# Self-attention with plain values and an output projection over all tokens, and the first cross attention's transposes of P by quarters

## The reference, cut to what matters

```
# layer 0, 16 heads of width 8, keys and values from a context of 77 rows
scores = einsum(Q, K) / 8**0.5, causal;  sim = softmax(scores);  att = einsum(sim, V)
x = LN(att + q);  x = x + gelu(x @ W1.T + b1) @ W2.T + b2

# layer 3, 16 heads of width 64
xn = rms_norm(x, attn_norm_w)
q, k, v = split(xn @ to_qkv_w);  q, k = rope(q), rope(k)
kf = [memory keys (16 equal ones), 16 persistent keys, k];  vf likewise
mask: a token sees memory and persistent keys, and the tokens before it in its own segment of 64
o = softmax(q kf^T / 8) vf
x = x + concat_heads(o) @ to_out_w          # 1024 x 128
```

## Time and profile before

| | us |
|---|---|
| median of 3 runs | 2436.97 (2435.53 to 2437.94) |
| the profiled execution | 2442.62 |
| its span in the profile | 2440.8 |

### The profile page before, as it was taken

One profiled execution on the slowest core, in us unless ns is written; L12 is line 12 of the kernel. 1 busy time (PEld: TensorE's weight loads), 2 busy tenths in 40 slices (PEclk: granted clock), 3 DMA queues, 4 the chain that ended last, 5 costly groups with the idle time before them and its releaser, 6 DMA issues.

```text
span 2440.8 us, 83677 instructions
## 1 busy us (share of the span) xinstructions
PE 2287.5 (94%) x27182; PEld 1807.3 (74%) x27182; DVE 1872.0 (77%) x4067; ACT 1474.2 (60%) x3344; POOL 1562.2 (64%) x2374
## 2 busy tenths in 40 slices
PE   7999999988888888999999979999999999999899
PEld 5777778976666666777778967777777777777688
DVE  5888882149999996777775678888888888888566
ACT  5777775548888886888885524444444444444443
POOL 2666663119999995666667766666666666666433
PEclk9999999979999998999999989999999999999999
DMA  4111112235555552222222223333333333333221
GB/s 128 43 43 43 43 45 63 71 90 167 168 167 168 167 157 47 52 50 52 52 50 58 69 72 93 94 96 97 95 94 95 94 94 94 94 94 93 61 62 54
DMA packets 443188, 211.72 MB, mean 87 GB/s; under 512 B 206672, under 2 KB 434000, under 8 KB 442960
## 3 DMA queue, kind: packets, MB, share of 16 engines
q1 hardware_dynamic: 443088, 210.43, 31.9%
HBM read 113.28 MB, written 29.88 MB: 59 GB/s over the span
## 4 chain that ended last, share of the span: by engine, by line
PE 70%; POOL 12%; issue 8%; ACT 4%; DVE 2%; SPq 1%; DMA 1%; POOLq 0%; DVEq 0%; ACTq 0%
PE bank L685 10%; PE bank L1458 9%; PE bank L1418 9%; PE bank L1149 6%; PE bank L702 5%; PE bank L1486 5%; PE bank L659 4%; PE bank L1163 4%; POOL sb_region L1008 4%; ACT sb_pT L771 3%; PE bank L1468 3%; PE bank L1444 3%; POOL sb_rstd L1025 2%; PE bank L1494 2%; POOL sb_z L1029 2%
## 5 line engine op out<-in xcount | busy, mean ns | idle before, releaser
L685 PE MATMUL bank<-sb_ident,sb_region 128*77 128x128 f32 x3072 | 413.0, 278 | 54.0 <-ACT sb_pT L771 50.7
L771 ACT ACTIVATE sb_pT<-bank 77x1024 f32<-77x1024 f32 x384 | 391.8, 1020 | 83.3 <-PE bank L685 82.5
L685 PEld LDWEIGHTS bank<-sb_ident,sb_region 128*77 128x77 f32 x3072 | 349.8, 151 | 107.7 <-issue 104.0
L1548 ACT ACTIVATE sb_l<-sb_l 128x640 f32<-128x640 f32 x128 | 94.5, 738 | 386.6 <-DVE sb_l L1596 386.6
L862 DVE TENSOR_REDUCE sb_max<-bank 128x8 f32<-128x616 f32 x256 | 203.4, 795 | 143.3 <-PE bank L667 74.5
L766 ACT ACTIVATE sb_region<-sb_region 128x616 f32<-128x616 f32 x384 | 276.6, 721 | 22.3 <-POOL sb_region L1008 20.7
L1675 POOL TENSOR_TENSOR sb_pn<-sb_l,sb_r_all 128x512 f32<-128x512 f32 x128 | 134.8, 1053 | 233.0 <-DVE sb_r_all L1606 222.0
L1418 PE MATMUL bank<-sb_region,sb_wqkv 128*128 128x128 f32 x2048 | 253.5, 277 | 6.2 <-DVE sb_region L1584 5.5
L1418 PEld LDWEIGHTS bank<-sb_region,sb_wqkv 128*128 128x128 f32 x2048 | 241.8, 194 | 8.8 <-DVE sb_region L1584 6.1
L1458 PE MATMUL bank<-sb_wvo,sb_region 128*64 128x512 f32 x1024 | 247.9, 605 | 0.0
L867 DVE TENSOR_TENSOR sb_region<-bank,sb_max 128x616 f32<-128x616 f32 x256 | 204.8, 800 | 11.7
(11 more groups left out here) (181 smaller groups left out, 5434.6 us busy)
## 6 DMA issues: line engine op xcount, KB each, us to landing
sb_region<-in_side SPq DMA_DIRECT2D x64, 616.0 KB, 3.8
sb_pT<-sb_region SPq DMA_DIRECT2D x512, 64.0 KB, 2.0
sb_kF<-sb_region SPq DMA_DIRECT2D x512, 64.0 KB, 2.1
scratch_after_A<-sb_y SPq DMA_DIRECT2D x256, 64.0 KB, 1.7
sb_fx<-scratch_after_A SPq DMA_DIRECT2D x96, 128.0 KB, 2.1
sb_mask<-in_mask SPq DMA_DIRECT2D x64, 154.0 KB, 2.3
sb_x<-scratch_after_F SPq DMA_DIRECT2D x128, 64.0 KB, 1.9
sb_ctx<-in_ctxT SPq DMA_DIRECT2D x192, 38.5 KB, 1.8
```

Of the source, the lines that this page charges most:

```text
L685: mm = nc.tensor.transpose(two[0:C, h * T:(h + 1) * T], p_s[b.par][:, head * C:(head + 1) * C], ident[:])
L771: nc.scalar.activation(pT_s[k][:], two[0:C, :], ACT.Copy).then_inc(pT_kept.sem(b), 1)
```

## The change

**A3.** The values are no longer folded with the output weights. `values` is now v = xn Wv for one segment g of all 16 heads: two matmuls of 512 columns in a half instead of four. `attend_local` multiplies v with transposed P for every head and segment apart: 16 matmuls of 64 rows, 64 weight columns and 64 moving columns, into banks 0 and 1, and gives O^T. ACT copies it (`keep_outputs`), and `project_local` multiplies it with `wout3`, in four matmuls over all 128 tokens that accumulate in `out3_bank`. The heads of the two row groups of an odd c land in the other half of the partitions, and so `wout3_turned`, loaded once, holds those rows turned. The output of a half is now taken one half later (the project of (b-1, h) stands in the step of (b, h)). The rope's banks are 3 and 6 instead of 0 and 1. The triangle mask is added by two matmuls over all 128 rows of output instead of four. The norm's weight is applied when xT is copied; SP loads `vom` and the residual for b instead of b+1 and stores y of b-2 instead of b-1.

**The memory stage** loses the eight transposes of Wv, both `fold_values`, and DVE's copies of them. **A0**: each half of P is transposed and copied by quarters of four heads, each quarter in a bank of its own with semaphores `quarter_made` and `quarter_kept`. A1 and A2 keep the halves.

```
@@ events
-        pT_made = event("pT_made", CROSS, parts=2)
-        pT_kept = event("pT_kept", CROSS, parts=2)
+        pT_made = event("pT_made", CROSS[1:], parts=2)
+        pT_kept = event("pT_kept", CROSS[1:], parts=2)
+        quarter_made = event("quarter_made", ["A0"], parts=4)
+        quarter_kept = event("quarter_kept", ["A0"], parts=4)
@@ A0, PE
+            def transpose_quarters(b, k):
+                pe.wait_ge(exp_made.sem(b), exp_made.count(ph, b, k))
+                for q in range(2):
+                    old, old_k = (b, 0) if k == 1 else (b + -1, 1)
+                    if old.exists:
+                        pe.wait_ge(quarter_kept.sem(old), quarter_kept.count(ph, old, 2 * old_k + q))
+                    for h in range(QH):
+                        head = (2 * k + q) * QH + h
+                        mm = nc.tensor.transpose(bank[4 + q][0:C, h * T:(h + 1) * T], p_s[b.par][:, head * C:(head + 1) * C], ident[:])
+                    mm.then_inc(quarter_made.sem(b), 1)
@@ A0, ACT
+            def keep_quarters(b, k):
+                wait_earlier(act, att_made, ph, b, 1, k)
+                for q in range(2):
+                    act.wait_ge(quarter_made.sem(b), quarter_made.count(ph, b, 2 * k + q))
+                    nc.scalar.activation(pT_s[k][:, q * QH * T:(q + 1) * QH * T], bank[4 + q][0:C, :], ACT.Copy).then_inc(quarter_kept.sem(b), 1)
@@ A3, banks
-        rope_bank = bank[0:2]
+        rope_bank = (bank[3], bank[6])
-        vo_banks = (bank[6], bank[3])
+        oT3_banks, v3_bank = bank[0:2], bank[1]
@@ A3, SP
-                if has(1):
-                    load_vom(b + 1)
-                    load_residual(b + 1)
-                if has(-1):
-                    sp.wait_ge(out3_taken.sem(b + -1), out3_taken.count(ph3, b + -1, 1))
+                if has(0):
+                    load_vom(b)
+                    load_residual(b)
+                if has(-2):
+                    sp.wait_ge(out3_taken.sem(b + -2), out3_taken.count(ph3, b + -2, 1))
@@ A3, PE
+            def values(b, g, first):
+                done, done_h = (b + -2, 1) if g == 0 else (b + -1, 0)
+                if done.exists:
+                    pe.wait_ge(oT3_kept.sem(done), oT3_kept.count(ph3, done, done_h))
...
                 for r in range(2):
-                    mm = nc.tensor.matmul(vo_banks[g][r * SEG:(r + 1) * SEG, :], xnT_s[b.lap][:, g * SEG:(g + 1) * SEG],
-                                          wvo[:, (2 * h + r) * HC * D:(2 * h + r + 1) * HC * D], start=True, stop=True)
+                    mm = nc.tensor.matmul(v3_bank[r * SEG:(r + 1) * SEG, :], xnT_s[b.lap][:, g * SEG:(g + 1) * SEG], wv3[:, r], start=True, stop=True)
+            def outputs_ready(b, h, held):
+                for v, g in held:
+                    pe.wait_ge(v3_kept.sem(v), v3_kept.count(ph3, v, g))
+            def attend_local(b, h):
+                for c in range(HC):
+                    for r in range(2):
+                        rows = slice(r * KH, (r + 1) * KH)
+                        side = (r + c) % 2
+                        for g in range(T // SEG):
+                            tok, col, out = c * T + g * SEG, (g * (H // 2) + h * HC + c) * KH, (c // 2 * 2 + g) * SEG
+                            mm = nc.tensor.matmul(oT3_banks[c % 2][side * KH:(side + 1) * KH, out:out + SEG], v3_s[b.par][rows, col:col + KH],
+                                                  pT_s3[h][rows, tok:tok + SEG], start=True, stop=True)
+                mm.then_inc(oT3_made.sem(b), 1)
+            def project_local(b, h, leaving):
...
+                if leaving:
+                    late, late_h = (b, 1) if h == 0 else (b + 1, 0)
+                    pe.wait_ge(pp3_kept.sem(late), pp3_kept.count(ph3, late, late_h))
...
                 for c in range(HC):
+                    weights = wout3[:, h * HC + c, :] if c % 2 == 0 else wout3_turned[:, (h * HC + c) // 2, :]
+                    tok = (c % 2 * (HC // 2) + c // 2) * T
+                    nc.tensor.matmul(out3_bank[:, 0:D], oT3_s[h][:, tok:tok + T], weights, start=(c == 0), stop=False, skip_group_check=True)
@@ A3, ACT
             def step(b, has):
                 for h in range(2):
+                    if has(-1):
+                        keep_outputs(b + -1, h)
                     if has(0):
                         exps(b, h)
                     if has(-1) if h == 0 else has(0):
                         keep_p(*half_before(b, h))
-                    if has(0):
-                        keep_values(b, h, 0)
-                        keep_values(b, h, 1)
+                    if has(0) if h == 0 else has(1):
+                        keep_values(b + h, 1 - h)
@@ memory stage, PE
-            for c in range(H // 2):
-                col = 2 * HD3 + c * 128
-                mm = nc.tensor.transpose(bank[4 + c // 4][:, (c % 4) * 128:(c % 4 + 1) * 128], wqkv[:, col:col + 128], ident[:])
-            pe.wait_ge(wvT_kept, 2)
-            fold_values(0)
-            pe.wait_ge(wvo_kept, 1)
-            fold_values(1)
```

More of the change, by code:

```diff
@@ L1413, in project @@
                 for eo in range(2):
+                    if b.first and what == "q" and eo == 1:
+                        last = Batch(GROUPS // 2 - 1, 1)
+                        pe.wait_ge(ft_made.sem(last), ft_made.count("F2", last))
                     if old.exists:
@@ L1511, in step @@
                         project(b + 2, "qk"[h])
-                    if has(0):
-                        values(b, h, 0)
-                        values(b, h, 1)
-                    if leaving:
-                        attend_local(old, old_h)
+                    if has(0) if h == 0 else has(1):
+                        values(b + h, 1 - h, not has(-1))
+                    if has(-1):
+                        project_local(b + -1, h, leaving)
                     following = (b, 1) if h == 0 else (b + 1, 0)
@@ L1633, in step @@
                 for h in range(2):
-                    if has(-1):
-                        take_out(b + -1, h)
+                    if has(-2) if h == 0 else has(-1):
+                        take_out(*((b + -2, 1) if h == 0 else (b + -1, 0)))
                     if h == 0 and has(3):
@@ L1730, in build_layers @@
         rest = [(dst[:], src) for dst, src in consts]
+        by_row = a[p + "to_out_w"].rearrange("(c odd r v) d -> odd r v c d", odd=2, r=2, v=KH)
+        for r in range(2):
+            rest.append((wout3_turned[r * KH:(r + 1) * KH, :, :], by_row[1, 1 - r]))
         for r in range(2):
```

140 lines of the change are left out of this document (68 added, 72 removed).

## The result

The changed kernel takes 2527.99 us (median of 3 runs, 2523.56 to 2532.52) against 2436.97 us (2435.53 to 2437.94): ratio 1.0364, 95% interval 1.0344 to 1.0384. It is 91 us slower where 32 us faster was forecast, and outside of the range. Its profiled execution has a span of 2526.2 us.

The account below looks back on a forecast made before the run. TensorE's own work was taken to bound A3, with SP next, and waits and a POOL chain A0. A3 -16.5, A0 -12.5, memory stage -5, A1 and A2 +2 sum to -32 us: median 2405, range 2388 to 2428.

Parts of the forecast that it names:

- The failed step: A3: TensorE's own work sets the time, so each microsecond taken from it counts 64 times until something else is late.
- Rival (1): A3: a run of four on one tile in attend_local holds the queue, 1.48 us, 2501 in all; chance 8%.
- Rival (3): A3 gains next to nothing, as v3_kept or the late rope puts back 0.15 us per half; 2422; chance 17%.
- A3's own gain: Self-attention: 13.03 us per batch, 0.30 less, for 62 batches, -18.5, plus 2 at the end: -16.5 us.
- The deeper pipeline's tail: End of A3: the last half's copy (0.60) and projection (0.94) stand bare with their latencies: +2 us.
- The wait on pp3_kept stays covered by 0.3: A3, per half: values end at 4.97 us, the transposed persistent part is kept at 4.67, so no wait.
- The rope and v3_kept: A3: the rope's 0.46 us delay fits DVE's 0.54 idle; project_local's 0.94 covers the 0.92 v3_kept wait, almost bare.
- A0: First cross attention: quarters remove the transposes' wait; the scores-to-scores chain over POOL sets 5.38 us, 0.2 less per batch: -12.5 us.
- The memory stage: Both folds go: -3.3 us for the first, -1.5 for the second, together -5, bounds -8 and -2.
- A1 and A2: Second and third cross attention: same work, two more register instructions per batch on ACT in each: +2 us, bounds 0 and +6.
- SP's 12.98: A3: SP issues 20 DMAs per batch in 12.98 us and can't go much lower, the next limit after TensorE.
- Same-bank pairs: A3, attend_local: row tiles writing one PSUM bank take turns, 0.95 us, 2433 in all; a rival at 6%.

Follow-up runs that it names:

- slot 0: Changed kernel with only TensorE's code moved, the self-attention loop's head at the first of a block's 256 instruction places: 2425.06 us, ratio 0.9937 to the kernel before.
- the run without waits: Changed kernel at slot 0, ScalarE's copies of the transposed probabilities put ahead of the exponentials: 2420.30 us, ratio 0.9912 to the kernel before.
- the run with the hint: Changed kernel, loop not placed, with a hint at the body's head announcing its closing branch to the instruction fetch: 2422.84 us, ratio 0.9916 to the kernel before.
- the last version: Changed kernel with branch hint, probability copies ahead of exponentials, and the self-attention mask again in four pieces of 64 partitions: 2417.19 us, ratio 0.9911 to the kernel before.
- slots 0 and 88: Changed kernel with only the loop's head placed, at instruction 0 or 88 of a block: 2425.06 and 2424.34 us, ratios 0.9937 and 0.9934 to the kernel before.
- slot 104: Changed kernel with only the loop's head placed, at instruction 104 of a block: 2468.71 us, ratio 1.0075 to the kernel before.
- the lengthened old one: Kernel before plus 14 superfluous matmuls per self-attention half: 2489.55 us (1.0191) with the loop's head at slot 0, 2584.02 us (1.0573) at slot 239.

## Why the prediction was wrong

**The failed step** is in the part on A3, and it is one that is not there. It says "each microsecond taken from it counts 64 times, until something else is late", and lists as what could be late SP, ScalarE's copies and the ropes. The instructions themselves are not in the list. The change's count of records was worked out for their duration (32 for attend_local, 8 for the projection, half of the values) and never added up as code. The sum was at hand: 170 records per batch before are 170 products and as many weight loads, and 36 more of each come to 72 x 4 = 288 instructions per pass, on top of 1,427 (the trace has 269 more, since other instructions fell away). What the profile before would have shown is its queue list: 57 code packets in all, none in A3's passes, so the loop was being replayed from what the engine holds. How much it holds no row before shows. The Trainium skill does, in Runtime: NRT & Kernel Launch, section Instruction fetch mechanics: 128 KiB for TensorE, 2,048 instructions, refilled in blocks of 16 KiB, and a taken branch to a block outside of a window of two stops the engine until that block is fetched. The runs agree with the capacity and the block: 7 blocks are held, 8 are at the edge. They disagree with the window of two blocks: at slot 0 a body of 7 blocks is replayed for 12 passes without a packet. By the capacity the changed loop with its 1,696 instructions would have looked safe; that it isn't hangs on where its head stands.

What the runs showed in the place of that step: the loop's code is fetched anew in every pass, at 8.6 us per pass, and the same operations at slot 0 take 2425.06 us where they took 2527.99, 103 us less. That is still outside of the range: 17 us under the kernel before and not 32, for the sizes told of next.

**Rival (1)**, slower by a run of four in attend_local (2501), had the sign and not the mechanism: attend_local takes 0.69 us. **Rival (3)**, A3 gains next to nothing (2422), has about the time of the runs without fetches, by chance: neither v3_kept nor the ropes took the gain.

**A3's own gain**, apart from the fetches, was forecast as -16.5 and is about zero. Three sizes were off. (a) Per half, values and attention together were to go from 2.74 to 2.57; the sections of the run without waits are 0.687 for attend_local (0.70 forecast), 1.009 for half of the values (0.89), 0.995 for the projection (0.94): 2.69. The values' four records cost 0.25 each and not 0.22, and the first two of the projection 0.33 and not 0.22. Both stand at a change of tile shape, for which I had 0.04 in all, and only for another place; no run changes the shape alone, so that this is the cause is a reading. (b) The new mask, two pieces for four, was put at nothing: 0.215 + 0.611 for mask and scores against 0.133 + 0.664, 0.03 more per half. Against this the persistent part (L1493 and L1494 before) fell from 0.97 to 0.81 us per batch, which the sum didn't have. In all TensorE's own work fell from 13.31 to 13.12 us per batch where 12.99 was forecast. So a pass is 52.5 to 52.7 instead of 4 x 13.03 = 52.1, and 12 passes gain 5.6 us. (c) The deeper pipeline's tail was to cost 2 and costs 4 to 5. TensorE's waits in it in the run with the hint (2194 to 2307), in total, times, longest:

```profile
PE bank L1541 <- ACT sb_ppT L1603: 3.3, 2, 2.2
PE bank L1541 <- ACT sb_ppT L1605: 3.2, 3, 1.2
PE bank L1508 <- issue: 1.7, 1, 1.7
```

The copies of the persistent part stop TensorE for 6.5 us against 4.9 before, and the stop for code is the 1.7. At slot 0 the copies are 6.0, and two more stops (3.3 in all) stand in front of L1546, where the code waits for SP's gathers. In the last version the end of A3 takes 7.8 us more than before, 3.5 of them in one wait for gathered keys.

**The covers.** "The wait on pp3_kept stays covered by 0.3" was wrong: in the run at slot 0 the copy lands 0.05 before the projection starts, and TensorE waits for it in both halves, 0.05 us per batch in all. The rope and v3_kept did hold, with no wait of TensorE on either.

**A0** was right in mechanism and nearly in size: -12.5 forecast, -13.9 measured alone, by the closed chain over POOL. In the traces a pass of four batches went from 22.06 to 21.22 us, 0.21 less per batch, for 0.2; the levels are both 0.1 under those of the prediction, since the trace has somewhat fewer records than the program. **The memory stage**: -5 forecast, -5.9 measured (-5.3 from its first matmul to A1's first). **A1 and A2**: +2 forecast, +1.5 measured. **SP's 12.98** was right as a floor, though in the loop only the last run reaches it.

**Same-bank pairs.** The rule that was weighed against L667 does not hold for this pattern: attend_local writes one bank from two row groups, and takes 0.69 us and not the 0.95 of turns.

## What to carry to other kernels

Count the instructions of a loop's body on each engine, weight loads included, before and after a change that trades a few long operations for many short ones, and look at the instruction queue's row: a loop that is replayed without a packet has a property that can be lost. If TensorE has idle time marked "issue" once per pass, directly behind the loop's branch, and the queue that brings the code has packets in every pass, it is the code and not the data. "Issue" alone is not the mark: the stops at L1546 had it and were waits for gathered keys. The place of the loop's head took the stops away here without touching an operation, and so did a hint for its branch. Short matmuls of another tile shape seem to have a price at each change of shape (here about 0.1 us), which can eat what fewer columns bring.

## What the runs showed of the hardware that was not expected

- TensorE replayed a body of 1,696 instructions from what it holds when this lay in 7 blocks of 256 (slots 0 and 88), fetched all of it in 5 of 12 passes when it reached 8 slots into an eighth (slot 104), and in every pass where it reached 147 slots into it (the head at slot 243 by the distance of the two stops). One block too many costs all blocks.
- The cost was 8.6 us per pass of 52.7 in the changed kernel and 8.2 in the lengthened old one: in the pass shown two stops of 3.4 and 2.7 us, and then 5 us with the granted clock at 0.57.
- A hint for the branch made a body, most likely in 8 blocks, replay without a packet; leaving the loop then cost one stop of 1.7 us (2.8 in the last version).
- 14 superfluous matmuls of 16 columns cost 0.43 us per half, (56.7 - 53.3) / 8, which is 0.03 us each.
- Two bf16 matmuls of 256 columns that write 128 partitions took 0.215 us where four that write 64 each took 0.133, at twice the instructions.
